# Two-block transformer kernel: attention constants made in the second group from rounded parts instead of in the head from f32

## The reference, cut to what matters

```python
# block 0: s is the recurrent layer, which reduces to one 256x256 matrix M
xi = xn @ W_in.T ; y = sum(C_real*B_real*xi - C_imag*B_imag*xi) ; out = y @ W_out.T
s = xn + rmsnorm(out, norm_w)
# block 1: s is causal attention over a second, scaled norm
q, k, v = (x_norm @ qkv[:, 0:256]), (x_norm @ qkv[:, 256:512]), (x_norm @ qkv[:, 512:768])
attn = softmax(where(causal, (q @ k.T) / 16, -inf))
s = (attn @ v) @ o_proj + xn
# both: ffn
hidden = fwht(silu(xn @ W1.T) * (xn @ W3.T)) ; ffn = hidden @ W2.T
```

## Time and profile before

| | |
|---|---|
| median of 3 runs | 357.87 us (357.84 to 357.94) |
| the profiled execution | 357.93 us |
| its span, first to last instruction | 356.1 us |
| TensorE busy | 350.6 us (98%) |
| VectorE busy | 248.8 us (70%) |
| ScalarE busy | 167.5 us (47%) |
| GpSimd busy | 105.2 us (30%) |

### The profile page before, as it was taken

One profiled execution on the slowest core, in us unless ns is written; L12 is line 12 of the kernel. 1 busy time (PEld: TensorE's weight loads), 2 busy tenths in 40 slices (PEclk: granted clock), 3 DMA queues, 4 the chain that ended last, 5 costly groups with the idle time before them and its releaser, 6 DMA issues.

```text
span 356.1 us, 4969 instructions
## 1 busy us (share of the span) xinstructions
PE 350.6 (98%) x1785; PEld 297.9 (84%) x1785; DVE 248.8 (70%) x482; ACT 167.5 (47%) x326; POOL 105.2 (30%) x122
## 2 busy tenths in 40 slices
PE   7999999999999999999999999999999999999996
PEld 4887888888888888888988879888888888888896
DVE  5679964995499667956498874887547886356645
ACT  2865442446254724363465634654346544464510
POOL 2164410456036934662024030240300603004000
PEclk9999999999999999999999999999999999999999
DMA  7999679215150303130351302606014251054001
GB/s 244 242 188 229 157 111 123 64 40 129 53 129 17 111 12 106 35 117 0 120 148 39 112 0 83 179 18 197 2 59 147 62 159 49 14 177 130 5 3 59
DMA packets 69648, 34.44 MB, mean 97 GB/s; under 512 B 40692, under 2 KB 69624, under 8 KB 69624
## 3 DMA queue, kind: packets, MB, share of 16 engines
q1 hardware_dynamic: 69480, 34.06, 37.9%
q10 hardware_dynamic: 144, 0.07, 0.1%
HBM read 21.99 MB, written 12.12 MB: 96 GB/s over the span
## 4 chain that ended last, share of the span: by engine, by line
PE 96%; DVE 2%; DMA 1%; POOL 0%; issue 0%; ACT 0%
PE GU L358 20%; PE GU L360 20%; PE GU L359 20%; PE O L358 8%; PE O L359 8%; PE O L360 8%; PE O L426 1%; PE T L358 1%; DMA X<-in_L_attn_x 1%; PE T L360 1%; PE T L359 1%; PE O L509 1%; PE O L508 1%; PE O L507 1%; PE T L365 1%; PE O L365 1%
## 5 line engine op out<-in xcount | busy, mean ns | idle before, releaser
L722 ACT ACTIVATE hf<-GU 128x512 f32<-128x512 f32 x64 | 38.2, 599 | 80.5 <-DVE hid L842 63.0
L998 DVE TENSOR_TENSOR hf<-hf,GU 128x512 f32<-128x512 f32 x64 | 43.5, 679 | 30.0 <-PE GU L360 24.1
L842 DVE TENSOR_TENSOR hid<-hf,hid 128x512 fp32r<-128x512 f32 x64 | 51.2, 801 | 0.3
L358 PE MATMUL GU<-XT,W1T 128*128 128x512 f32 x128 | 50.5, 395 | 0.0
L360 PE MATMUL GU<-XT,W1T 128*128 128x512 f32 x128 | 49.9, 390 | 0.0
L359 PE MATMUL GU<-XT,W1T 128*128 128x512 f32 x128 | 49.9, 390 | 0.0
L358 PE MATMUL GU<-XT,W3T 128*128 128x512 f32 x128 | 49.8, 389 | 0.0
L360 PE MATMUL GU<-XT,W3T 128*128 128x512 f32 x128 | 49.8, 389 | 0.0
L359 PE MATMUL GU<-XT,W3T 128*128 128x512 f32 x128 | 49.8, 389 | 0.0
L358 PE MATMUL O<-hid,W2hi 128*128 128x512 f32 x112 | 43.9, 392 | 0.0
L359 PE MATMUL O<-hid,W2hi 128*128 128x512 f32 x112 | 43.7, 390 | 0.0
(11 more groups left out here) (205 smaller groups left out, 729.8 us busy)
## 6 DMA issues: line engine op xcount, KB each, us to landing
swap_rows<-GX SPq DMA_DIRECT2D x7, 512.0 KB, 3.3
sT<-swap_rows SPq DMA_DIRECT2D x28, 128.0 KB, 2.7
swap_gate<-GX SPq DMA_DIRECT2D x7, 512.0 KB, 2.9
sT<-swap_gate SPq DMA_DIRECT2D x28, 128.0 KB, 2.7
stage<-in_L_ffn_W SPq DMA_DIRECT2D x12, 256.0 KB, 4.3
swap_p<-PX SPq DMA_DIRECT2D x4, 640.0 KB, 3.2
PL<-swap_p SPq DMA_DIRECT2D x16, 160.0 KB, 3.1
stage<-in_L_ffn_W SPq DMA_DIRECT2D x32, 64.0 KB, 2.6
```

Of the source, the lines that this page charges most:

```text
L358: pe.matmul(o, lhs(0), rhs(0), start=start, stop=False)
L722: act.activation(hf[:, c % 2, :], GU[:, c % 2, 0, :], ACT.Silu).then_inc(silu_done, 1)
L842: dve.tensor_tensor(dst, src, hi_part.bitcast(F32), ALU.subtract).then_inc(done, 1)
L998: dve.tensor_tensor(hf[:, c % 2, :], hf[:, c % 2, :], GU[:, c % 2, 1, :], ALU.mult).then_inc(mul_done, 1)
```

## The change

`small_av` leaves the head and stands behind up chunk 1 of group 1 on TensorE. It no longer reads f32 operands: ScalarE makes rounded parts wqkvH (three activations) and woH (one), VectorE the parts wqkvL and woL (four subtractions), and TensorE makes each constant by `mm3`, so 24 matmuls in place of 8 f32 ones. `turn_wqkv` and these parts go to the start of group 1: on ScalarE behind `squares`, ahead of `x_hi`; on VectorE behind `recurrent_scale`, ahead of `x_lo`. The splitting of the two results moves to chunk 2 on ScalarE and behind `turn_w2` of chunk 3 on VectorE. TensorE's wait for sm_lo 3 moves ahead of `next_hadamard`, which uses the same bank T. The new tiles lie where the head's tiles and, from there on, W1T1 and W3T1 lie.

```diff
--- before.py
+++ after.py
@@ -110,8 +110,6 @@
         W1T0 = sb("W1T0", [P, 2, KC, H], F32R)
         W3T0 = sb("W3T0", [P, 2, KC, H], F32R)
         with ExitStack() as early:
-            win = sb("win", [P, MC, D], F32, early)
-            woutT = sb("woutT", [P, MC, D], F32, early)
             wo = sb("wo", [P, KC, D], F32, early)
             wqkvT = sb("wqkvT", [P, 3, KC, D], F32, early)
             ssm = sb("ssm", [P, 5, MC, DS], F32, early)
@@ -119,6 +117,13 @@
             kvec = sb("kvec", [P, MC], F32, early)
             gbrow = sb("gbrow", [2 * KC, P], F32, early)
             mask = sb("mask", [P, P], F32, early)
+            wqkvH = sb("wqkvH", [P, 3, KC, D], F32R, early)
+            woH = sb("woH", [P, KC, D], F32R, early)
+            with ExitStack() as earlier:
+                win = sb("win", [P, MC, D], F32, earlier)
+                woutT = sb("woutT", [P, MC, D], F32, earlier)
+            wqkvL = sb("wqkvL", [P, 3, KC, D], F32R, early)
+            woL = sb("woL", [P, KC, D], F32R, early)
         W1T = (W1T0, sb("W1T1", [P, 2, KC, H], F32R))
         W3T = (W3T0, sb("W3T1", [P, 2, KC, H], F32R))
         U, U2, W2hi, W2lo = [], [], [], []
@@ -189,6 +194,7 @@
         wout_loaded, wqkv_loaded, wo_loaded = sem("wout_loaded"), sem("wqkv_loaded"), sem("wo_loaded")
         wout_turned, wqkv_turned, win_scaled = sem("wout_turned"), sem("wqkv_turned"), sem("win_scaled")
         xnext_loaded = sem("xnext_loaded")
+        av_hi, av_lo = sem("av_hi"), sem("av_lo")
         w2_loaded, w2_turned = sem("w2_loaded"), sem("w2_turned")
 
         w_tr, w2_tr, w_hi, w_lo = sem("w_tr"), sem("w2_tr"), sem("w_hi"), sem("w_lo")
@@ -429,18 +435,14 @@
 
             def small_av():
 
-                pe.wait_ge(wqkv_turned, 3)
-                pe.wait_ge(wo_loaded, 16)
-                for i in range(KC):
-                    for c in range(KC):
-                        last = pe.matmul(T[:, 0, i * D:(i + 1) * D], wqkvT[:, 0, c, i * P:(i + 1) * P], wqkvT[:, 1, c, :],
-                                         start=(c == 0), stop=(c == KC - 1))
-                last.then_inc(sm_mm, 1)
-                for i in range(KC):
-                    for c in range(KC):
-                        last = pe.matmul(T[:, 1, i * D:(i + 1) * D], wqkvT[:, 2, c, i * P:(i + 1) * P], wo[:, c, :],
-                                         start=(c == 0), stop=(c == KC - 1))
-                last.then_inc(sm_mm, 1)
+                pe.wait_ge(av_lo, 4)
+                qkv2, wo2 = (wqkvH, wqkvL), (woH, woL)
+                for q in (0, 1):
+                    for i in range(KC):
+                        for c in range(KC):
+                            rhs = (lambda a: qkv2[a][:, 1, c, :], lambda a: wo2[a][:, c, :])[q]
+                            last = mm3(T[:, q, i * D:(i + 1) * D], lambda a: qkv2[a][:, 2 * q, c, i * P:(i + 1) * P], rhs, c == 0, c == KC - 1)
+                    last.then_inc(sm_mm, 1)
 
             def first_x_transposes():
 
@@ -550,10 +552,8 @@
                 up_chunk(0, 0, 6, True)
                 small_m()
                 up_chunk(0, 0, 7, True)
-                small_av()
                 pe.wait_ge(sm_lo, 1)
                 recurrent_mix(0)
-                pe.wait_ge(sm_lo, 3)
 
             def block0_group(n):
                 if n == 1:
@@ -562,9 +562,12 @@
                     down_chunk(0, n - 1, i)
                 for c in range(HC):
                     up_chunk(0, n, c, False)
+                    if c == 1 and n == 1:
+                        small_av()
                     if c == 1 and n > 1:
                         next_hadamard(PAIRS + 2 * n - 3)
                 if n < 3:
+                    pe.wait_ge(sm_lo, 3)
                     next_hadamard(PAIRS + 2 * n - 2)
                 recurrent_mix(n)
 
@@ -763,7 +766,6 @@
                 w2_hi(0)
                 chunk(0, 7, True)
                 hid_hi_chunk(0, 7)
-                small_hi([(flat[1], T[:, 0, :]), (flat[2], T[:, 1, :])], 2, sm_mm, 2, sm_hi)
                 act.wait_ge(mask_loaded, 16)
                 act.activation(identR[:, :], ident[:, :], ACT.Copy).then_inc(const_ready, 1)
                 act.activation(maskR[:, :], mask[:, :], ACT.Copy).then_inc(const_ready, 1)
@@ -771,11 +773,17 @@
             def block0_group(n):
                 act.wait_ge(hid_ready, 8 * n)
                 squares(n - 1)
+                if n == 1:
+                    for w in range(3):
+                        hi(wqkvH[:, w, :, :], wqkvT[:, w, :, :], wqkv_turned, w + 1, av_hi)
+                    hi(woH[:, :, :], wo[:, :, :], wo_loaded, 16, av_hi)
                 x_hi(n)
                 gate(n - 1)
                 act.wait_ge(ssq_ready, 4 * n)
                 for c in range(HC):
                     chunk(n, c, False)
+                    if c == 2 and n == 1:
+                        small_hi([(R[:, 0, :, :].rearrange("p k d -> p (k d)"), T[:, q, :]) for q, R in enumerate((AR, VR))], 2, sm_mm, 2, sm_hi)
                     if c == 2 and n > 1:
                         pair_u(1, PAIRS + 2 * n - 3, 2 * n - 3)
                     if c == 3 and n < 3:
@@ -1024,6 +1032,9 @@
                         turn_w(PAIRS + 2 * n - 2)
                     if c == 3:
                         turn_w2(2 * n - 2)
+                        if n == 1:
+                            small_lo(1)
+                            small_lo(2)
                     if c == 6:
                         turn_w(PAIRS + 2 * n - 1)
                     if c == 7:
@@ -1098,7 +1109,6 @@
                 chunk(0, 5)
                 x_turn(1)
                 chunk(0, 6)
-                turn_wqkv()
                 w2_sums(0)
                 small_lo(0)
                 w2_lo(0, 0)
@@ -1106,12 +1116,15 @@
                 w2_lo(0, 1)
                 dve.wait_ge(xrest_loaded, 16)
                 dve.wait_ge(small_loaded, 16 * N_SMALL)
-                small_lo(1)
-                small_lo(2)
                 hid_lo_chunk(0, HC - 1)
 
             def block0_group(n):
                 recurrent_scale(n - 1)
+                if n == 1:
+                    turn_wqkv()
+                    for w in range(3):
+                        lo(wqkvL[:, w, :, :], wqkvT[:, w, :, :], wqkvH[:, w, :, :], av_hi, w + 1, av_lo)
+                    lo(woL[:, :, :], wo[:, :, :], woH[:, :, :], av_hi, 4, av_lo)
                 x_lo(n)
                 gate_flip(n - 1)
                 for c in range(HC):
```

## The result

| | before | after |
|---|---|---|
| median of 6 runs | 357.90 us | 361.07 us |
| range | 357.80 to 358.36 | 360.88 to 362.63 |
| profiled execution, its span | 357.93, 356.1 | 360.88, 359.1 |
| TensorE busy | 350.6 us | 351.1 us |

The ratio is 1.0100, with an interval of 1.0078 to 1.0121: 3.2 us slower, against 2.9 us forecast. Four of the six executions lie between 360.88 and 361.10 with a mean granted clock of 1.000, two at 362.55 and 362.63 with 0.995; the last experiments are about these.

A forecast was written before the change was run, and what follows sets the result against it. TensorE, busy 98% of the span, was taken to bound the kernel. -0.34 at the up chunk, +2.88 for small_av and +0.4 at the Hadamard matmul gave 360.8 us from 357.93; own range 360.2 to 361.4 (68%), wider 359.5 to 362.0.

The forecast's parts named there:

- Columns: TensorE, small_av: 24 fp32r matmuls at 0.12 us, 2.88 us, replace the head's 3.45; 0.57 us back from matmul work alone.
- The turn gives nothing in the head: VectorE, head: removing turn_wqkv (1.81 us) gains nothing, since w2_sums waits for GpSimd's butterfly and still ends at 40.92.
- The chain: Second group, hid_ready 8 through rms and recurrent_scale to x_lo: 54.89 - 1.20 + 1.81 + 2.40 = 57.90 us.
- The hole: TensorE, second group's first up chunk: arrives at about 55.4, waits about 2.5 us for x_lo, restarts at 58.0.
- ScalarE beside it: ScalarE, start of second group: four high parts, 2.1 us, run beside VectorE's work and cost nothing, ending at about 55.5.
- The Hadamard matmul: Second group: nat_lo comes 1.09 us later relative to TensorE against 0.75 of room; with the hand-over about 0.4 us.
- The sum: Whole kernel: -0.34 + 2.88 + 0.4 = +2.9 us, from 357.93 to 360.8 us.
- the first term: TensorE's restart at the second group's first up chunk, 58.0 against 58.34 before: -0.34 us.
- The hole was there: Rival, 6%: XT of the second group is split by 54.9, no wait at the up chunk, 357.4 us.
- w2_sums didn't come earlier: Rival, 12%: VectorE and GpSimd run side by side from 37.5, the wait shrinks 0.5 to 1.4 us, 359.5 to 360.3.
- The third: Rival, 7%: after the 2.5 us wait TensorE runs at 1.2 GHz, costing 1.9 us, 362.7 us.
- the further 3% beyond the range: Chance given beyond the 359.5 to 362.0 us range, besides the first and the third rival.

The follow-up runs named there:

- the last experiments: The changed kernel rerun as control (ratio 1.0104), with ten unused matmuls filling TensorE's wait (1.0087), and with four more VectorE subtractions ahead of x_lo (1.0212).
- the version with everything moved: Changed kernel's three-term products with turn, parts, small_av, result splitting and small_lo(0) all placed beside waits, against the kernel before: 357.62 us, ratio 0.9988.

## Why the prediction was right

- *Columns.* The slot of small_av is 66.21 - 63.35 = 2.86 us (forecast 2.88), against 3.45 in the head. The matmuls have the 0.12 us of the recurrent mix.
- *The turn gives nothing in the head.* Right: w2_sums ends at 40.74 (40.9 forecast), with the forecast record of 3.4 us, and putting the turn back costs nothing.
- *The chain.* hid_ready 8 came 1.4 us earlier than before (45.64 + 0.69 against 47.69) where 1.20 was forecast; 0.18 of it is a head that ran so much earlier in this execution. From recurrent_scale to the end of x_lo it took 57.71 - 49.34 = 8.37 us, forecast 57.90 - 49.51 = 8.39. The hole: 2.4 us, forecast 2.5.
- *ScalarE beside it.* Right: its high parts end at 55.3, half a microsecond ahead of the low part that needs the last.
- *The Hadamard matmul.* A wait with hand-over of 0.36 us (82.89 - 66.21 - (80.10 - 63.78)), and 0.08 more to the mix. Forecast 0.4.
- *The sum.* -0.58 + 2.86 + 0.15 at the restart + 0.44 = 2.87 at the mix of group 1, 3.0 in the span. The last 0.1 us came later and is not explained. That this lies so near the 2.94 forecast is in part luck: the first term came out 0.24 better than the -0.34 forecast, most of it by the early head of this execution, and the 0.15 us that the two chunks behind the hole take longer was in no term.
- *The rivals.* The hole was there, and w2_sums didn't come earlier. The third, at 7%, was undersized: the lower clock behind the hole is there in a third of the executions, at 362.6 (forecast 362.7). I had weighed it as a thing that happens or doesn't; it happens now and then, and in these runs more often behind a longer hole. My ground against it, that the hole is short with dense matmuls on both sides, didn't hold. Its price of 1.9 us rested on the distances of the first matmuls alone: the granted clock in the profile before reads 1.00 from 1 to 5 us, where they stand. The price measured, between the two groups of executions of the changed kernel, is 1.5 to 1.8.
- *The chances.* The forecast and its rivals make 100% together (68, 6, 12, 7, 7), so the further 3% beyond the range had no share left.

## What to carry to other kernels

Moving work off the engine that bounds a kernel is worth what the work took only if no wait of that engine loses its cover: here 3.45 us went from TensorE's head and 0.57 of columns was all there was to win, while 4.2 us of preparation were put into the one serial stretch that the next stage waits for. Put preparation for a product where its engine waits for another (the rms of GpSimd, the butterfly that blocks VectorE), and read the slack of every hand-over from the trace before the move. A hole in TensorE's matmuls costs its length, and at the 2.4 us and more of these runs sometimes the clock behind it as well; between 0.6 and 2.4 us nothing was measured.

## What the runs showed of the hardware that was not expected

- A wait of TensorE of 2.4 us is followed in some executions (4 of 12) by a lower mean clock and a time 1.5 to 1.8 us longer; with 2.9 us in 3 of 5, with 5.2 us in 4 of 4. The two traces that hold such an execution show a stretch at 1.2 GHz, whose level fell 2.8 us after the last matmul in one and 4.8 us in the other.
- A VectorE sum of two SBUF tensors of 1024 columns took 1.20 us alone (in the version with everything moved), 1.60 when it started 0.5 us ahead of the end of GpSimd's butterfly, and 3.41 when it started 2.3 us ahead. Each time it ended 1.1 us behind the butterfly (40.92 against 39.83 before, 40.74 against 39.65 after), so its record includes the time in which it did nothing.
